# Graph attention, 8 heads over 4096 nodes: the two halves of a head's output are summed and scaled on GpSimd instead of VectorE

## The reference, cut to what matters

```python
def gnn(h, adj, Wks, Wqs, Wvs, Wo):           # h: 4096 x 256, 8 heads of 64
    adj = jnp.maximum(adj, eye)
    q, k, v = (jnp.einsum('nd,hdk->hnk', h, W) for W in (Wqs, Wks, Wvs))
    scores = jnp.einsum('hqk,hmk->hqm', q, k) * kd ** (-0.5)
    scores = scores + 0.01 * eye - 1e16 * (1.0 - adj)
    att = jax.nn.softmax(scores, axis=-1)
    return jnp.einsum('hqm,hmk,hko->qo', att, v, Wo)

h = jnp.maximum(layernorm(x), 0.0)
x = x + gnn(h, adj, Wks, Wqs, Wvs, Wo)
```

## Time and profile before

| | |
|---|---|
| three runs | 2649.67, 2654.58, 2655.53 us; median 2654.58 |
| profiled execution | 2653.47 us, span 2651.3 us, mean granted TensorE clock 0.997 |
| PE busy | 2602.6 us, 98% of the span |
| DVE busy | 2254.8 us, 85% |
| ACT busy | 1844.9 us, 70% |
| POOL busy | 1284.1 us, 48% |

### The profile page before, as it was taken

How to read it: one execution, slowest core, us unless ns; L and a number is a source line. 1 busy time by engine, 2 the same in 40 slices (tenths; PEclk the granted TensorE clock), 3 DMA queues, 4 the chain that set the end, 5 groups by cost and what they waited for, 6 DMA issues and landing times.

```text
span 2651.3 us, 58401 instructions
## 1 busy us (share of the span) xinstructions
PE 2602.6 (98%) x17344; PEld 1900.8 (72%) x17344; DVE 2254.8 (85%) x3833; ACT 1844.9 (70%) x3041; POOL 1284.1 (48%) x2424
## 2 busy tenths in 40 slices
PE   7999999999999999999999999999999999999997
PEld 5777777777767777777767777777777777777775
DVE  7888888888888888888848888888888888888885
ACT  4677677776766767767737777677777767777774
POOL 3355655556565555565413443434444343444443
PEclk9999999999999999999999999999999999999999
DMA  6477877677778667787644565666556565565564
GB/s 182 123 162 169 189 180 179 171 160 180 167 178 187 174 167 166 168 190 178 155 144 120 137 151 143 169 146 156 146 136 150 145 170 143 158 149 134 146 148 106
DMA packets 264000, 419.06 MB, mean 158 GB/s; under 512 B 100032, under 2 KB 121024, under 8 KB 259840
## 3 DMA queue, kind: packets, MB, share of 16 engines
q1 hardware_dynamic: 174176, 231.24, 34.3%
q0 software_dynamic: 89760, 187.05, 30.8%
HBM read 136.84 MB, written 46.27 MB: 69 GB/s over the span
## 4 chain that ended last, share of the span: by engine, by line
PE 82%; DMA 5%; SPq 5%; DVE 4%; issue 2%; POOL 1%; DVEq 0%; ACT 0%; POOLq 0%
PE psS L486 30%; PE psO L523 15%; PE psO L509 15%; PE psT L499 15%; SPq L265 5%; DMA S<-S 4%; PE psS L440 2%; DVE S L763 2%; PE psP L165 2%; PE psP L471 2%; DVE S L784 1%; PE psP L459 1%; PE psO L459 1%; POOL S L324 1%; DMA rden_scratch<-rden 0%
## 5 line engine op out<-in xcount | busy, mean ns | idle before, releaser
L324 POOL DMA_DIRECT2D S<-S x2048 | 1007.5, 500 | 1101.3 <-DVE S L784 1050.8
L763 DVE CUSTOM_DVE_ANT_0 S<-psS,B 128x1024 f32<-128x1024 f32 x1024 | 1227.7, 1219 | 218.1 <-PE psS L486 140.8
L642 ACT ACTIVATE S<-S,negm 128x1024 f32<-128x1024 f32 (+1 forms) x768 | 1095.9, 1428 | 44.4 <-DVE negm L770 43.9
L649 ACT ACTIVATE PT<-psT 128x512 f32<-128x512 f32 x1024 | 594.8, 596 | 254.5 <-PE psT L499 235.9
L486 PE MATMUL psS<-K,QH 128*128 128x512 f32 x2048 | 725.4, 435 | 14.0 <-DVE mx L763 13.3
L486 PE MATMUL psS<-K,QL 128*128 128x512 f32 x2048 | 640.6, 394 | 0.0
L784 DVE STREAM_TRANSPOSE S<-S 128x2048 f32<-128x2048 f32 x256 | 590.4, 2306 | 37.2 <-PE psO L523 33.8
L499 PEld LDWEIGHTS psT<-ident,S 128*128 128x128 f32 x4096 | 480.5, 140 | 185.9 <-issue 73.1
L499 PE MATMUL psT<-ident,S 128*128 128x128 f32 x4096 | 606.6, 276 | 2.9 <-ACT PT L649 2.9
L509 PE MATMUL psO<-PT,V 128*64 128x256 f32 x4096 | 492.1, 382 | 0.0
L523 PE MATMUL psO<-S,V 128*64 128x256 f32 x4096 | 472.9, 384 | 4.4 <-DMA S<-S 4.4
(11 more groups left out here) (51 smaller groups left out, 971.1 us busy)
## 6 DMA issues: line engine op xcount, KB each, us to landing
S<-S SPq DMA_DIRECT2D x2048, 64.0 KB, 3.2
S<-S POOLq DMA_DIRECT2D x2048, 64.0 KB, 3.0
B<-in_adj POOLq DMA_DIRECT2D x128, 256.0 KB, 7.1
bias_scratch<-B SPq DMA_DIRECT2D x32, 1024.0 KB, 5.3
B<-bias_scratch SPq DMA_DIRECT2D x128, 256.0 KB, 4.2
hq<-hT_scratch SPq DMA_DIRECT2D x32, 256.0 KB, 4.7
RB<-rden_scratch SPq DMA_DIRECT2D x128, 64.0 KB, 3.4
S<-in_x SPq DMA_DIRECT2D x8, 512.0 KB, 3.8
```

The costliest lines, as they stand in the source:

```text
L324: pool.dma_start(dst, src).then_inc(late_sent[q][half], 16)
L642: nc.scalar.activation(part, part, ACT.Exp, bias=negm[:, h % 2, q:q + 1], accum_out=sums[:, h % 2, q, e:e + 1]).then_inc(probs_ready, 1)
L649: nc.scalar.activation(PT[:, s % RING, :], psT[s % 2][:, :], ACT.Copy).then_inc(pt_act, 1)
L763: nc.vector.tensor_tensor_reduce(out=part, in0=psS[j % 2][:, :], in1=B[:, q, k * SLOT:(k + 1) * SLOT], scale=SCALE, scalar=LOWEST, op0=ALU ...
```

## The change

DVE's `sum_halves` goes. ACT copies both halves of psO, the upper into Oodd, the lower straight into the head's rows of O. A new `sum_halves` on GpSimd adds them in place, and multiplies in place by RB. Oodd and RB get 128 partitions, so that heads with even and odd h have rows of their own. TensorE's first `values` of a step waits for the copies (o_copied) and no longer for the sum; ACT's copies wait in addition for the projection that reads O. On GpSimd the sum of the last head stands behind the step's second lot of moves (and behind the loads of the h = 2 step that follow them), ahead of the store and of the last conversions; the sum of a group's last head stands ahead of `load_next_group`.

```diff
@@ sync_program, step
-            sp.dma_start(RB[:, :], rden_scratch[h % 2].rearrange("p q -> (p q)").partition_broadcast(KD)).then_inc(rden_in, 16)
+            rows = slice(h % 2 * KD, (h % 2 + 1) * KD)
+            sp.dma_start(RB[rows, :], rden_scratch[h % 2].rearrange("p q -> (p q)").partition_broadcast(KD)).then_inc(rden_in, 16)
@@ gpsimd_program
+        def sum_halves(i, h):
+
+            rows = slice(h % 2 * KD, (h % 2 + 1) * KD)
+            wait_apart(pool, o_copied, count(i, h, 1, 1 + START), pool_passed)
+            nc.gpsimd.tensor_tensor(O[rows, :], O[rows, :], Oodd[rows, :], ALU.add).then_inc(o_summed, 1)
+            wait_apart(pool, o_summed, count(i, h, 1, 1), pool_passed)
+            wait_apart(pool, rden_in, count(i, h, 16, 16), pool_passed)
+            own = O[rows, :].rearrange("k (q p) -> k q p", q=QT)
+            nc.gpsimd.tensor_tensor(own, own, RB[rows, :].rearrange("k (p q) -> k q p", q=QT), ALU.mult).then_inc(o_ready, 1)
+            wait_apart(pool, o_ready, count(i, h, 1, 1 + START), pool_passed)
...
                 for k in range(2):
                     load_adj(i + 1, 1, k)
+            if prev or h:
+                sum_halves(*last_step(i, h))
             if prev and h == 1:
                 store(i - 1)
                 load_base(i)
...
         for h in range(GROUP):
             step(PAIRS - 1, h, False, True, 0)
+        sum_halves(PAIRS - 1, GROUP - 1)
         if g + 1 < GROUPS:
             load_next_group()
         store(PAIRS - 1)
@@ tensor_program, values
             if s == 0:
-                pe.wait_ge(o_summed, count(i, h, 1, START))
+                pe.wait_ge(o_copied, count(i, h, 1, START))
@@ scalar_program, step
             act.wait_ge(o_ready, count(i, h, 1, START))
-            nc.scalar.activation(Oodd[:, :], psO[KD:2 * KD, 0:QW], ACT.Copy).then_inc(odd_copied, 1)
+            act.wait_ge(projected, count(i, h, 1, START - h % 2))
+            rows = slice(h % 2 * KD, (h % 2 + 1) * KD)
+            nc.scalar.activation(Oodd[rows, :], psO[KD:2 * KD, 0:QW], ACT.Copy)
+            nc.scalar.activation(O[rows, :], psO[0:KD, 0:QW], ACT.Copy).then_inc(o_copied, 1)
@@ vector_program
-        def sum_halves(i, h):
-
-            dve.wait_ge(odd_copied, count(i, h, 1, 1))
-            nc.vector.tensor_tensor(Oodd[:, :], psO[0:KD, 0:QW], Oodd[:, :], ALU.add).then_inc(o_summed, 1)
...
                 mask(i1, h1, 3)
-            if prev:
-                sum_halves(*last_step(i, h))
             if nxt:
                 mask(i1, h1, 4)
...
         steps(dve, step)
-        sum_halves(PAIRS - 1, GROUP - 1)
         add_heads(PAIRS - 1, GROUP - 1)
@@ build
-        Oodd = sb("Oodd", [KD, QW])
-        RB = sb("RB", [KD, QW])
+        Oodd = sb("Oodd", [P, QW])
+        RB = sb("RB", [P, QW])
```

More of the change, by code:

```diff
@@ L94, in group_programs @@
     if not norm:
-        late_used_before, late_moved_before, late_sent_before, slot_masked_before, projected_before, o_summed_before, head_added_before, bias_kept_before, pt_free_before, project_before, next_w_before, next_h_before = before
+        late_used_before, late_moved_before, late_sent_before, slot_masked_before, projected_before, o_copied_before, head_added_before, bias_kept_before, pt_free_before, project_before, next_w_before, next_h_before = before
     heads = slice(g * GROUP, (g + 1) * GROUP)
@@ L121, in group_programs @@
      transposed, pt_act, pt_free, o_ready, projected, summed, den_ready, head_added,
-     late_transposed, late_used, odd_copied, o_summed, rden_stored, rden_in) = (
+     late_transposed, late_used, o_copied, o_summed, rden_stored, rden_in) = (
         sem(f"{s}{g}") for s in (
@@ L125, in group_programs @@
             "probs_ready", "transposed", "pt_act", "pt_free", "o_ready", "projected", "summed", "den_ready",
-            "head_added", "late_transposed", "late_used", "odd_copied", "o_summed",
+            "head_added", "late_transposed", "late_used", "o_copied", "o_summed",
             "rden_stored", "rden_in"))
@@ L358, in gpsimd_program @@
         pool.sem_inc(res_free, START)
+        pool.sem_inc(o_ready, START)
         if norm:
@@ L448, in value_rows @@
                 if not norm:
-                    pe.wait_ge(o_summed_before, STEPS + START)
+                    pe.wait_ge(o_copied_before, STEPS + START)
                     pe.wait_ge(head_added_before, STEPS + START)
@@ L692, in scalar_program @@
         act.sem_inc(pt_act, PT_START)
+        act.sem_inc(o_copied, START)
         value_rows(EARLY)
@@ L867, in vector_program @@
         dve.sem_inc(head_added, START)
-        dve.sem_inc(o_summed, START)
-        dve.sem_inc(o_ready, START)
         if norm:
@@ L886, in vector_program @@
         steps(dve, step)
-        sum_halves(PAIRS - 1, GROUP - 1)
         add_heads(PAIRS - 1, GROUP - 1)
     return ((sync_program, gpsimd_program, tensor_program, scalar_program, vector_program),
-            (late_used, late_moved, late_sent, slot_masked, projected, o_summed, head_added, bias_kept, pt_free,
+            (late_used, late_moved, late_sent, slot_masked, projected, o_copied, head_added, bias_kept, pt_free,
              lambda pe: project(pe, PAIRS - 1, GROUP - 1), next_w, next_h))
```

## The result

The changed kernel takes 2692.62 us in the median of four runs, the kernel before 2652.12 beside it: ratio 1.0152, 95% interval 1.0136 to 1.0169, 40.5 us slower. The forecast was 2685 with a range of 2665 to 2700. The profiled execution took 2691.17 us with a span of 2688.9, 37.6 us over the span before.

A forecast was written before the change was run, and what follows sets the result against it. The prediction took TensorE to bound the kernel, so time freed on DVE buys nothing. It summed 2653.5 + 18.6 (h = 3 steps) + 11.5 (between groups) + 1.2 (end) = 2684.8, say 2685 us, range 2665 to 2700.

The forecast's parts named there:

- What bounds the kernel: Whole kernel: TensorE is the bound; DVE time taken away buys nothing in group 1, at most 11.35 us in group 0.
- The rival that TensorE's modelled busy time hides waits for DVE: Every step: DVE's freed 0.83 us comes back up to 128 times, 106 us, so not slower; 6%.
- The price on GpSimd: GpSimd, per head: two operations of 0.75 us and two waits of 0.19, 1.88 us in all (1.24 to 2.1).
- the rival that the conversions stay covered: Group 0, h = 3: conversions cost nothing, only the start of group 1 and the end do; 2666 us; 8%.
- the one with 4 us per head: GpSimd's sum far dearer, say 4 us per head; h = 3 steps lose 3.4 us each; 2719 us; 8%.
- The estimate by the Trainium skill alone: GpSimd's sum from the skill page's figures: 0.55 us for 256 columns, 1.5 us per head.
- The h = 3 steps: Group 0: sum delays conversions, masks 6 and 7 come 1.35 us late; 15 steps lose 1.3 us each, 18.6 net.
- The h = 2 steps: Group 0: the 1.88 us sum fits in GpSimd's 2.64 us of idle time, so no cost.
- Between the groups: Before group 1's keys: the sum delays the prefetch, TensorE begins 11.5 us late, all exposed (7.3 to 16).
- The end: After the last head: the exposed chain to TensorE's projection grows by 1.2 us (0.6 to 2).
- The total: Whole kernel: terms add 31.3 us to 2653.5, giving 2684.8, say 2685 us.

The follow-up runs named there:

- run 4: Changed kernel with group 1's loads issued before the last head's sum, and GpSimd's add and multiply left out with the waits between them: 2652.77 us, ratio 0.9996.
- run 1: Changed kernel with GpSimd's sum moved behind the last two conversions in group 0's h = 3 steps: 2670.5 us, ratio 1.0073.
- run 5: Changed kernel with one more add of the same shape on GpSimd between its add and its multiply: 2718.09 us, ratio 1.0258.
- run 6: Changed kernel with conversions and group 1's loads ahead of the sum, plus six extra GpSimd adds behind each sum in group 1: 2666.75 us, ratio 1.0062.
- run 7: Kernel before, group 1's loads split: weights and first 512 rows early, other three row loads after the last head's moves landed: 2650.05 us, ratio 0.9998.
- run 2: Changed kernel with GpSimd issuing the loads for group 1 ahead of the last head's sum: 2679.85 us, ratio 1.0103.
- run 3: Changed kernel with both the last two conversions (h = 3, group 0) and group 1's loads put ahead of the sum: 2654.33 us, ratio 1.0010.

## Why the prediction was right, and where it was off

**What bounds the kernel.** Right. Group 1, without conversions, is as long as before with 40 us less on DVE and 90 us more on GpSimd, and run 4 puts the worth of DVE's 0.83 us per head at nothing. The rival that TensorE's modelled busy time hides waits for DVE is refuted. In group 0, where the freed time could have given back 11.35 us at most, run 1 shows the h = 3 steps 1.8 us shorter than in the kernel before and the h = 0 steps 0.7 longer.

**The price on GpSimd.** The operations were sized right, the waits too small. Groups by line in the changed kernel:

```profile
L347 POOL TENSOR_TENSOR O<-O,RB 64x256 f32<-64x256 f32 x128 | 94.4, 738 | 42.9 <-POOL O L343 42.9
...
L343 POOL TENSOR_TENSOR O<-O,Oodd 64x256 f32<-64x256 f32 x128 | 93.5, 730 | 23.2 <-ACT O L695 15.8
```

0.73 and 0.74 us, against 0.75. The multiply, with its stride of two in RB, takes 8 ns more than the add. But between the two stand two waits, not one (for the sum and for the denominators), and 42.9 / 128 = 0.34 us; behind the multiply 0.30. The whole is 2.14 us where I put 1.88, a little over the upper bound of 2.1. That puts out the rival that the conversions stay covered, which needed under 0.55 us, and the one with 4 us per head. The estimate by the Trainium skill alone (GPSIMD Engine Reference, section Performance versus the Vector engine), 1.5 us per head, was further off; a fixed part does come on top of its 2.6 cycles an element, 0.73 us for the add where that figure alone is an estimate of 0.55.

**The h = 3 steps.** The mechanism is shown, by undoing it in run 1. The term was 18.6 us and measured 21.6. Two sizes were off: 0.26 us of waits on GpSimd, and 0.29 us from the end of the first conversion (557.47 + 2.05 / 2 = 558.50) to DVE's mask 6 at 558.79, which I had put at 0.1. Mask 6 came 1.76 us late (10.82 after the step's start, 9.06 before) and not 1.35; mask 7 then followed it without the gap that it had before, so the step lost 1.5 us, not 1.3.

**The h = 2 steps.** I had them at nothing, and the 2 us of sum fit there: the moves that follow start no later relative to the step. The profile shows 4.1 us more. But the same fifteen steps came out between 318.6 (run 5) and 324.8 us (run 6) over the seven kernels with the sum at this place, with no relation to the edits. Their mean is 321.8, where the two kernels with the sum on DVE have 319.2 and 319.1. So more than half of the 4.1 us may belong to the change, and nothing here shows how; each kernel has one profiled execution. About 1.2 of the 4.1 us fell in cycle 8 alone, where TensorE waited 2.25 us for a mask and then ran at a granted clock of 0.53.

**Between the groups.** 11.5 us forecast, 15.0 - 4.0 = 11.0 measured, but that is luck: two errors cancel. The late loads cost more than I took: the first rows landed 8.5 us after their issue (7.2 taken), the loads were issued 0.6 us after the sum's end, and the matmuls behind the idle time were slowed by the clock, 5.46 - 3.70 = 1.8 us. On the other side the last step of group 0 became 4.0 us shorter, as the loads no longer ran beside its moves. TensorE's timeline there, in the changed kernel:

```profile
1356.75 3.67 PE L539 MATMUL psO<-S,V 128*64 128x256 f32 x32 [1.87 <-DMA S<-S]
```

It waits 1.87 us in place of 3.35, and the matmuls behind take 3.67 us at a granted clock of 1.00 in place of 6.27 at 0.50. That this is the loads' doing is borne out by the runs: the step lasts 19.1 to 19.2 us in the three kernels that issue them right behind the last moves (before, runs 4 and 7, the last with a third of their bytes), 14.6 to 16.7 in runs 2, 3 and 6, which issue them 2.4 us later, and 14.7 to 15.2 in the three that issue them after the last head's sum (changed, runs 1 and 5). That the prefetch had a price of its own was nowhere in my sum.

**The end.** 1.2 us forecast, 1.5 measured.

**The total.** 31.3 us forecast, 37.7 in the profile, 40.5 between medians: the sum was short by 3 us in the h = 3 steps and by the 4 us of the h = 2 steps; the remaining 3 us lie between the profiled execution and the median of the runs.

## What to carry to other kernels

Moving work from an engine with little slack to one that is half idle costs nothing or much according to where it lands in that engine's queue: before moving it, list what stands behind the new place and who waits for that, conversions and prefetches above all. An engine that is 85% busy is not the bound if the steps are as long as another engine's work; take the work out altogether in one run, and see whether the time moves. Once the two things behind it were put ahead, this move was worth 0.1%, the wrong way and at the edge of what the runs can tell.

## What the runs showed of the hardware that was not expected

A wait of TensorE can cost more than its length: after 2.52 us of idle time the next matmuls ran at a granted clock of 0.62 in the mean (run 5, cycle 5), after 1.05 us at 1.00, after 13.50 us at 0.65, and an extra 0.73 us on GpSimd so became 1.9 us a step in the mean. It need not: behind a wait of 2.27 us (run 5, cycle 3) the clock stayed at 1.00. The levels are 1.2 and 2.4 GHz; a pair of score matmuls took 1.05 us in the slow stretch and 0.62 at full clock.

GpSimd can hold a DVE instruction. The timeline of DVE and of GpSimd in run 6:

```profile
2102.29 0.71 DVE L795 TENSOR_TENSOR S<-S,diag 128x128 f32 x1
...
2102.12 0.73 POOL L352 TENSOR_TENSOR Oodd<-O,Oodd 64x256 f32<-64x256 f32 x1 [0.18 <-POOL Oodd L352]
```

The add of the diagonal starts while a GpSimd add runs, which ends at 2102.85, and is done 0.15 us after that, 0.71 us for 0.29. The Trainium skill (SBUF — State Buffer, section Who interferes with whom) says that a DVE instruction with two SBUF inputs contends with a GpSimd instruction that reads SBUF, and that one with at most one SBUF input, outside the modes that use two ports, does not; both halves agree with these rows, since the mask, with one input in PSUM, kept its 1219 ns.
